# Four-bit stage: turning the weights inside the main block, and the order of the first silu

## The reference

```python
def fp4_quant_dequant(x):          # blocks of 16 along the last dimension
    xb = x.reshape(shape[:-1] + (shape[-1] // 16, 16))
    scale = jnp.maximum(jnp.max(jnp.abs(xb), axis=-1, keepdims=True) / 6.0, 1e-12)
    idx = jnp.searchsorted(_MID, jnp.abs(xb / scale))
    return (_GRID[idx] * jnp.sign(xb / scale) * scale).reshape(shape)

gate = fp4_linear(x, w_gate)       # both x and w go through fp4_quant_dequant
y = fp4_linear(x, w_up)            # w_gate, w_up: 704 x 256
h = jax.nn.silu(gate) * y
return fp4_linear(h, w_down)       # w_down: 256 x 704
```

## Time and profile before

| | |
|---|---|
| median of 3 runs | 2493.95 us (2488.51 to 2495.43) |
| the profiled execution, its own time | 2493.73 us |
| its span | 2492.0 us |
| busy: TensorE, VectorE, ScalarE, POOL | 95%, 72%, 52%, 28% |
| mean granted clock of TensorE | 0.971 |
| attention, until | 379.9 us |
| weights' block, until | 399.7 us |
| main four-bit block, until | 912.1 us |

### The profile page before, as it was taken

How to read it: one execution, slowest core, us unless ns; L and a number is a source line. 1 busy time by engine, 2 the same in 40 slices (tenths; PEclk the granted TensorE clock), 3 DMA queues, 4 the chain that set the end, 5 groups by cost and what they waited for, 6 DMA issues and landing times.

```text
span 2492.0 us, 43786 instructions
## 1 busy us (share of the span) xinstructions
PE 2357.8 (95%) x16024; PEld 2181.9 (88%) x16024; DVE 1785.5 (72%) x3323; ACT 1292.4 (52%) x2027; POOL 701.8 (28%) x468
## 2 busy tenths in 40 slices
PE   7999995999999969999999999998999999999999
PEld 6999994899999968898988988987988998899998
DVE  5776766899999857566566565565788887877774
ACT  4445543444444325455464464454666765655554
POOL 1110102454444423023023023123334442311110
PEclk9999996999999979999999999996999999999999
DMA  5000000000000000000000000011000010000001
GB/s 183 0 0 0 0 1 20 1 0 0 0 0 1 1 17 1 18 4 13 17 4 13 13 5 16 13 40 51 26 18 25 17 50 28 1 26 26 25 25 34
DMA packets 43259, 45.69 MB, mean 18 GB/s; under 512 B 3120, under 2 KB 41904, under 8 KB 43184
## 3 DMA queue, kind: packets, MB, share of 16 engines
q1 hardware_dynamic: 43184, 44.69, 5.6%
HBM read 27.90 MB, written 16.78 MB: 18 GB/s over the span
## 4 chain that ended last, share of the span: by engine, by line
PE 51%; DVE 6%; issue 3%; ACT 2%; POOL 1%; DVEq 0%; ACTq 0%; POOLq 0%
PE m_ps_z L1848 12%; PE p_ps_a L1630 5%; PE p_ps_feat L279 4%; PE p_ps_a L1687 4%; PE p_ps_feat L281 3%; PE p_ps_feat L280 3%; PE m_ps_wide L279 3%; PE m_ps_wide L281 3%; PE m_ps_wide L280 3%; PE p_ps_a L1568 2%; PE p_ps_turn L1674 2%; PE m_ps_wide L1826 1%; PE m_ps_wide L1827 1%; PE m_ps_n L1809 1%; PE p_ps_b L279 1%
## 5 line engine op out<-in xcount | busy, mean ns | idle before, releaser
L1940 DVE TENSOR_TENSOR m_a_lo<-m_a,m_a_hi 128x512 fp32r<-128x512 f32 x256 | 201.8, 805 | 144.5 <-ACT m_a_hi L1900 141.1
L1848 PE MATMUL m_ps_z<-m_w_hi,m_a_hi 128*128 128x256 f32 x1024 | 290.7, 284 | 1.5 <-DVE m_a_lo L1940 0.9
L1848 PE MATMUL m_ps_z<-m_w_hi,m_a_lo 128*128 128x256 f32 x1024 | 288.0, 281 | 0.0
L1848 PEld LDWEIGHTS m_ps_z<-m_w_hi,m_a_hi 128*128 128x128 f32 x1024 | 192.3, 188 | 13.5 <-DVE d_w_lo L2457 1.8
L1848 PEld LDWEIGHTS m_ps_z<-m_w_hi,m_a_lo 128*128 128x128 f32 x1024 | 192.8, 188 | 0.0
L1896 ACT ACTIVATE m_a<-m_ps_wide,d_b,d_w_gain 128x512 f32<-128x512 f32 x128 | 99.8, 780 | 135.7 <-PE m_ps_wide L281 131.7
L1313 POOL TENSOR_TENSOR p_kf<-p_kf,p_k_shift 128x1024 f32<-128x1024 f32 x64 | 119.4, 1903 | 155.5 <-DVE p_k_shift L1448 155.5
L1848 PE MATMUL m_ps_z<-d_w_lo,m_a_hi 128*128 128x256 f32 x512 | 144.7, 283 | 0.0
L1848 PE MATMUL m_ps_z<-m_w_lo,m_a_hi 128*128 128x256 f32 x512 | 143.6, 280 | 0.0
L1630 PE MATMUL p_ps_a<-p_ctx_pair,p_kf 128*128 128x34 f32 x1024 | 130.1, 285 | 0.0
L1630 PEld LDWEIGHTS p_ps_a<-p_ctx_pair,p_kf 128*128 128x128 f32 x1024 | 129.5, 205 | 0.4
(11 more groups left out here) (350 smaller groups left out, 8019.0 us busy)
## 6 DMA issues: line engine op xcount, KB each, us to landing
...
```

Source lines behind the costliest of these rows:

```text
L1848: mm = pe.matmul(z, a, w[:, f, :], start=(f == 0 and k == 0 and j % 2 == 0), stop=(f == FC - 1 and k == 2), skip_group_check=True)
L1940: dve.tensor_tensor(self.a2[1][:, f, :], self.a[f % RING][:, :], self.a2[0][:, f, :].bitcast(F32), ALU.subtract).then_inc(self.a_lo, 1)
```

## The change

- The last piece of the weights' rounding moves in between the attention's last tiles: its three parts run after the scores of tiles 4, 5 and 6.
- The moments of the last batch leave the attention. They are taken in step 5 of the four-bit pipeline on VectorE; POOL makes the root and the shift in step 8.
- The weights' block is gone. Its work is in the main block: TensorE turns the 8 wide pieces before the pipeline, in the banks of `gate` and `up`, and the 6 pieces of `down` after step 4, in the banks of h and `down`. ScalarE takes the high parts after steps 1, 3 and 5, and VectorE the low parts after steps 2, 3 and 5. The first products wait for them.
- In the steps while the pipeline fills, some engines have an order of their own (`fill`). TensorE makes `gate` and `up` of the first tile ahead of the transposes of n in steps 5 to 7; VectorE multiplies before it rounds h in step 6.
- In ScalarE's list, in every step, `gate(0)` stands ahead of `steps_h`.
- `performer_raw`'s loads and POOL's clearing of it wait until all weights are turned.

```diff
+        LAST_PIECE = {"s4": 0, "s5": 1, "s6": 2}
...
                     if e[0] in STEPS:
                         tile(b, STEPS[e[0]], int(e[1:]))
+                        if last and e in LAST_PIECE:
+                            tile(b, "fp4", LAST_PIECE[e])
...
-                if last:
-                    for m in range(len(FILLS)):
-                        beside(m)
-                else:
+                if not last:
                     projections(b + 1, 2, beside)
...
-            beside(B - 1)
+            fp4_weights.divide(pool, B - 1)
+            fp4_weights.restore(pool, B - 1)
...
     def step(self, s):
-        for g in range(len(self.groups)):
-            self.group(g, s)
+        if s in self.fill:
+            for lag, run in self.fill[s]:
+                run(s - lag, (s - lag) % self.unroll)
+        else:
+            for g in range(len(self.groups)):
+                self.group(g, s)
         if s in self.between:
             self.between[s]()
...
+        ps_w = [ps_gate[:, a, :] for a in range(2)] + [ps_up[:, a, :] for a in range(2)]
+        ps_w_down = [ps_h[:, a * D:(a + 1) * D] for a in range(4)] + [ps_down[:, a * D:(a + 1) * D] for a in range(2)]
+        WIDE_FILLS, FILLS = 4 * KD, 4 * KD + KF
...
+            sync.wait_ge(w_turned, FILLS)
             performer_raw.load(sync, dram)
...
-            performer_raw.clear(pool)
+            core.clear_finished(pool)
+
+            def clear_raw():
+                pool.wait_ge(w_turned, FILLS)
+                performer_raw.clear(pool)
+
+            def last_roots():
+                pool.wait_ge(last_var_ready, 1)
+                pool.tensor_tensor(core.rstd[:, last], last_var_eps[:, :], core.minus_half[:, :], ALU.pow).then_inc(last_rstd_ready, 1)
+                pool.wait_ge(last_rstd_ready, 1)
+                pool.tensor_tensor(core.shift[:, last], core.mean[:, last], core.rstd[:, last], ALU.mult).then_inc(last_rstd_ready, 1)
...
-            pipeline(pool, N, [(6, divide_h), (6, restore_h), (3, restore_n), (2, divide_n)], SLOTS)
+            pipeline(pool, N, [(6, divide_h), (6, restore_h), (3, restore_n), (2, divide_n)], SLOTS,
+                     between={7: clear_raw, 8: last_roots})
...
             pipeline(dve, N, [(8, add_down), (4, split_n), (7, split_h(0)), (3, round_n), (6, round_h), (5, multiply(0)),
-                              (7, split_h(1)), (2, scales_n), (5, multiply(1)), (5, scales_h)], SLOTS)
+                              (7, split_h(1)), (2, scales_n), (5, multiply(1)), (5, scales_h)], SLOTS,
+                     fill={5: [(4, split_n), (3, round_n), (5, lambda t, s: last_statistics()), (5, multiply(0)), (2, scales_n),
+                               (5, multiply(1)), (5, scales_h)],
+                           6: [(4, split_n), (3, round_n), (5, multiply(0)), (6, round_h), (2, scales_n), (5, multiply(1)), (5, scales_h)]},
+                     between={2: low_weights(0, 1, 2, 3), 3: low_weights(4, 5, 6, 7), 5: low_weights(*range(WIDE_FILLS, FILLS))})
...
-            pipeline(act, N, [(4, high_n), (7, high_h(0)), (3, steps_n), (6, steps_h), (5, gate(0)), (7, high_h(1)),
-                              (1, normalise), (5, gate(1))], SLOTS)
+            pipeline(act, N, [(4, high_n), (7, high_h(0)), (3, steps_n), (5, gate(0)), (6, steps_h), (7, high_h(1)),
+                              (1, normalise), (5, gate(1))], SLOTS,
+                     fill={6: [(4, high_n), (5, gate(0)), (3, steps_n), (6, steps_h), (1, normalise), (5, gate(1))]},
+                     between={1: high_weights(0, 1, 2, 3), 3: high_weights(4, 5, 6, 7),
+                              5: high_weights(*range(WIDE_FILLS, FILLS)), 9: lambda: act.wait_ge(last_rstd_ready, 2)})
...
+            def late(s):
+                return [(5, widen(0, 0)), (5, widen(0, 1)), (4, turn_n)] + [(7, turn_h(0)), (7, turn_h(1))][:2 * (s == 7)]
+
+            turn_weights(*range(WIDE_FILLS))
             pipeline(pe, N, [(4, turn_n), (7, turn_h(0)), (5, widen(0, 0)), (5, widen(0, 1)), (7, turn_h(1)),
-                             (5, widen(1, 0)), (7, narrow(0)), (5, widen(1, 1)), (7, narrow(1))], SLOTS)
+                             (5, widen(1, 0)), (7, narrow(0)), (5, widen(1, 1)), (7, narrow(1))], SLOTS,
+                     fill={5: late(5) + [(5, widen(1, 0)), (5, widen(1, 1))], 6: late(6) + [(5, widen(1, 0)), (5, widen(1, 1))],
+                           7: late(7) + [(5, widen(1, 0)), (7, narrow(0)), (5, widen(1, 1)), (7, narrow(1))]},
+                     between={4: lambda: turn_weights(*range(WIDE_FILLS, FILLS))})
```

110 lines of the change are left out of this document (61 added, 49 removed).

## The result

The changed kernel takes 2468.21 us (median of four runs, 2465.73 to 2468.78) where the kernel before, on the same chip, takes 2493.59 (2488.51 to 2495.43). The ratio is 0.990, interval 0.9886 to 0.9913: faster by 25.4 us. (All ratios and intervals here are those on record; they need not be the quotient of the two medians beside them.) The forecast was 2466 within 2459 to 2476. The profiled execution took 2467.79 us, its span is 2466.0, against 2493.73 and 2492.0 before.

A forecast was written before the change was run, and what follows sets the result against it. A ring through POOL, ScalarE's silu, TensorE and VectorE was taken to set the 14.86 us step. Fill 19.8 plus steady state 10.1 made 29.9, less 1.9 for the clock: 28.0 saved, so 2466 us, range 2459 to 2476.

The forecast's parts named there:

- Attention's tail: Last weights' piece moved between the last attention tiles: cost taken as 0, at most 3.0 us if VectorE's cover is gone.
- Hand-over: From attention's end to the four-bit stage: ScalarE's first normalisation starts at about 380.3, 20.0 us earlier.
- The fill: Pipeline start up to the third gated tile's scales: gains 19.8 us, table load and moments already paid.
- The walk: Six-point estimate of the fill; first three gated tiles' scales of h end at 410, 424.6 and 438.8.
- the clock's 1.9: TensorE in the fill: 1.9 us taken off for one or two batches at 1.2 instead of 2.4 GHz.
- the sixth point of the walk: Third gated tile in the fill: POOL, ScalarE and wake-ups 4.2 us, then rounding, products and scales, ending at 438.8.
- Table load: ScalarE's load before the first silu in the fill: bare in the new order, 1.28 us.
- Steady state: Silu before steps of h: 18 loop steps at 0.25, 8 written out at 0.4, 3 last at 0.8; together 10.1 us.
- The next late thing: Steady step: TensorE waits for VectorE's first product; VectorE's own gap before the second product is 0.35 in the loop.
- Drain: After the last gated tile: has no silu and stays as it was.
- Steady nothing: Rival: the steady step gains nothing because something unseen fills VectorE's gap; 2475.8 us, chance 0.12.
- Steps of h late behind the silu: Rival on ScalarE: late gate delays steps of h, lengthening all 29 steps; margin 0.5 us, 2505 at 1 us late, chance 0.03.

The follow-up runs named there:

- e1: The kernel before with one edit, gate(0) ahead of steps_h in ScalarE's list in every step; 2480.16 us, ratio 0.9958.
- e2: The changed kernel with steps_h put back ahead of gate(0) in ScalarE's list (only the fill's step 6 keeps its own order); 2480.25 us, ratio 0.9954.
- e4: The changed kernel with TensorE's order of step 7 alone put back, transposes of n and h ahead of the products; 2468.14 us, ratio 0.9905.
- e8: The changed kernel without VectorE's addition of the down product to x in the four-bit stage; 2474.0 us, ratio 0.9924.
- e7: The changed kernel with the last batch's moments ahead of split_n in VectorE's step 5; 2465.28 us, ratio 0.9891.
- e6: The changed kernel with VectorE's scales_n ahead of round_h in step 6; 2468.17 us, ratio 0.9896.
- e9: The changed kernel with an unused 128x1 silu on ScalarE in step 4, bringing the table load forward; 2465.43 us, ratio 0.9893.
- e11: The changed kernel once more without any edit, its second execution; 2473.15 us, ratio 0.9902.

## Why the prediction was right, by its own steps

The total was 25.9 us in the profiled execution against 28.0, and the mechanisms were the ones named. That the total came so close is in part luck: the drain gave 1.8 us that nobody forecast and that the second execution doesn't have, nearly what the steady state fell short by (1.9), and the total of one kernel moves between executions by more than this error of 2.1 us.

- **Attention's tail, 0.** The last update starts at 379.81, against 379.37. The attention's end lay between 379.6 and 382.8 over the changed kernels' executions and at 381.4 in e1, which has the old tail. So 0 within that spread.
- **Hand-over, 20.0.** The first normalisation at 380.60, forecast 380.3.
- **The fill, 19.8, less 1.9 for the clock.** Measured 16.6 and, in the second execution, 17.9. The walk gave the three marks at 30.2, 44.8 and 59.0 us after the attention's end (379.85); they came at 29.0, 44.7 and 62.2, and at 28.8, 44.6 and 60.9. The walk before its 1.9 can be held against steps taken each from an execution with the full clock from 10 us after the attention's end on: 28.1 (e2, e4, e8), 15.8 (step 6, the same in nearly all) and 14.5 (e7) make 58.4, a gain of 20.4. The walk had 30.2, 14.6 and 14.2 for these, so its 59.0 is right by errors that cancel. Step 5 came 2.1 us sooner: the walk gave `gate` and `up` of tile 0 half the lower clock, 5.9 us, and they ended at 394.9, not 396.8. Step 6 took 1.2 longer, of which e6 shows 1.0 to be VectorE's operation held beside POOL's restoring, which the walk didn't have. Against the 58.4 the clock took 3.8 us in the first and 2.5 in the second execution. **The mis-sized term is the clock's 1.9**, and behind it the sixth point of the walk (4.2 us from the scales to the rounding of h), which took 6.65 us: it counted POOL, ScalarE and the wake-ups and had nobody wait for TensorE. But ScalarE does its phases in order, the high parts of n and h stand ahead of the steps, and these wait for transposes that the new order put behind a late `up`. The new silu ahead of the steps stands in that row too.
- **Table load.** Forecast bare and 1.28 us; so it was, but at a full clock VectorE's moments hid it (28.2 in e9, 28.1 in e2, e4 and e8). The Trainium skill (ScalarE: Activation LUTs, What ACT_TABLE_LOAD costs) adds about 1380 ns of draining to the load. This trace disagrees: the load began 0.02 us after the steps ended, and the silu 0.01 us after the load.
- **Clock.** The granted clock was 0.66 over 396 to 406 and 0.68 over 420 to 436, after TensorE's waits of 3.36 and 3.38 us. So TensorE had its 1.2 GHz for part of these stretches and 2.4 for the rest. The Trainium skill (TensorE: Matmul & The Clock Gate, What's actually happening) says that the throttled state is the default; by this four slow bursts would have cost 8 us. The changed kernel's two executions show 2.5 to 3.8, and the other products-first ones less (e8 and e9: 1.1 and 1.2), because a slow burst counts only where VectorE or ScalarE waits for it.
- **Steady state, 10.1.** 8.2. In the loop 0.21 a step against 0.25 (14.849 to 14.638): 3.8 for 18 steps instead of 4.5. The last three gave 0.58 each instead of 0.8: 1.7 instead of 2.4. For the 8 written out that leaves 2.7 instead of 3.2. The next late thing, the order of the two waits and VectorE's gap (0.34, forecast 0.35) were right.
- **Drain, 0.** It gained 1.8, and 0.0 in e11. Over the changed kernels it took 20.5 to 22.3 us under the same code: not the change.
- **Rivals.** Steady nothing: refuted by e1. Steps of h late behind the silu: they still wait 0.78 us for POOL in the loop, so the margin of 0.5 held, with more room than forecast; but in step 7 of the fill, where `gate` and transposes are late, that rival's mechanism is real and cost a part of its 2.9 us (about 0.3 by e2 beside e8 and e9, at their clock), once instead of 29 times.

The rest differs with the places of TensorE's low clock. Held against each other instruction by instruction on VectorE, e11 fell 3.7 us behind the changed kernel between 150 and 157 us after the stage's end, where its clock was low from 150.7 to 157.5 and the changed kernel's was full. It lost 2.4 us more at each of two further such stretches (249.7 to 256.5 and 536.4 to 543.2), and won back 2.4 and 1.9 where the changed kernel had its own (341.0 to 347.8 and 627.7 to 631.1). From 700 us after the stage's end on the difference stays at 4.1 to 4.2. What puts the low clock in one place or another is open. Over 1030 to 1145 us, the changed kernel first, then e11:

```profile
1030.00:1145.00 115.00, 112.01 (x787) 100.76 (x786) 73.46 (x127) 61.63 (x84) 36.90 (x24) 1.00 0.03 9
```

```profile
1030.00:1145.00 115.00, 112.15 (x735) 99.92 (x734) 68.83 (x117) 58.70 (x81) 32.11 (x22) 0.94 0.03 9
```
